# Two attention steps as one period with three row-tiled stretches, seven PSUM banks in one pool, early loads, and softmax sums inverted behind their own load

## The reference

```
xn = layernorm(x)                                  # over 256 features
q, k, v = split(xn @ w_qkv + b_qkv)                # 16 heads of width 16
scores  = q k^T / 4,  kept only where key >= query # a causal mask turned round
s = softmax(scores) v, heads joined, @ w_out + b_out
h = relu(s0 * [xn, -xn] @ W0) * 2                  # W0, W1, W2 hold +1 and -1
h = relu(s1 * h @ W1) * 2                          # 1024 wide
g = silu(s2 * h @ W2)                              # back to 256 wide
out = x + s * g
```

## Time and profile before

| | us |
|---|---|
| median of the 3 timed runs | 2762.31 |
| lowest, highest | 2743.96, 2768.26 |
| the profiled execution | 2761.34 |
| its span, first to last instruction | 2758.0 |

### The profile page before, as it was taken

How to read it: one execution, slowest core, us unless ns; L and a number is a source line. 1 busy time by engine, 2 the same in 40 slices (tenths; PEclk the granted TensorE clock), 3 DMA queues, 4 the chain that set the end, 5 groups by cost and what they waited for, 6 DMA issues and landing times.

```text
span 2758.0 us, 51670 instructions
## 1 busy us (share of the span) xinstructions
PE 2505.2 (91%) x17604; PEld 1506.8 (55%) x17604; DVE 1842.7 (67%) x4506; ACT 1538.7 (56%) x3123; POOL 931.2 (34%) x1095
## 2 busy tenths in 40 slices
PE   5984889999999899999899999999999999999985
PEld 4773555555555555555555555555555555555542
DVE  7762677777777666767667677777666776767630
ACT  3550355666666565656656565656565565656452
POOL 4002332333333424333433334342434333342532
PEclk8996899999999999999999999999999999999996
DMA  6982011111111202121211213021212112120321
GB/s 210 347 334 71 12 29 35 40 36 44 31 45 35 81 26 75 40 76 37 60 48 44 75 31 88 25 73 40 75 40 57 48 44 75 37 82 22 88 87 60
DMA packets 158109, 193.44 MB, mean 70 GB/s; under 512 B 65328, under 2 KB 102064, under 8 KB 157872
## 3 DMA queue, kind: packets, MB, share of 16 engines
q1 hardware_dynamic: 156912, 190.29, 22.6%
q10 hardware_dynamic: 960, 0.00, 0.0%
HBM read 112.60 MB, written 76.55 MB: 69 GB/s over the span
## 4 chain that ended last, share of the span: by engine, by line
PE 75%; ACT 4%; DMA 4%; SPq 3%; DVE 3%; issue 2%; POOL 1%; ACTq 0%; POOLq 0%
PE b_ps L977 19%; PE b_pv_ps L955 18%; PE b_ps L924 16%; PE b_ps L936 10%; PE b_ps L974 5%; PE b_ps L981 5%; DMA b_heads_T<-heads_T 3%; PE b_ps L999 3%; ACT b_probs L1015 2%; DVE b_part_max L1069 2%; SPq L757 1%; ACT b_u L1043 1%; SPq L724 1%; ACT b_sig L1035 1%; ACT b_z L1036 1%
## 5 line engine op out<-in xcount | busy, mean ns | idle before, releaser
L1015 ACT ACTIVATE b_probs<-b_ps 128x512 f32<-128x512 f32 (+3 forms) x2560 | 1224.8, 532 | 799.6 <-PE b_ps L924 799.1
L1069 DVE TENSOR_REDUCE b_part_max<-b_ps 128x1 f32<-128x512 f32 x1536 | 984.5, 682 | 347.7 <-PE b_ps L936 341.7
L1066 DVE CUSTOM_DVE_ANT_0 b_ps<-b_ps,k_mask 128x512 f32<-128x512 f32 (+3 forms) x1024 | 484.6, 515 | 328.7 <-PE b_ps L936 326.9
L924 PE MATMUL b_ps<-b_qst,k_kst 50*128 50x512 f32 (+3 forms) x2560 | 604.8, 467 | 62.4 <-ACT b_probs L1015 58.4
L955 PE MATMUL b_pv_ps<-b_probs,k_vst 128*32 128x512 f32 (+3 forms) x5120 | 616.1, 554 | 4.5 <-POOL b_probs L841 4.3
L924 PEld LDWEIGHTS b_ps<-b_qst,k_kst 50*128 50x128 f32 x2560 | 248.0, 186 | 630.2 <-ACT b_probs L1015 493.4
L936 PE MATMUL b_ps<-k_kst,b_qst 48*128 48x512 f32 (+3 forms) x2560 | 503.8, 385 | 82.6 <-DVE b_part_max L1069 61.1
L977 PE MATMUL b_ps<-b_u_hi,k_w 128*128 128x256 f32 x2048 | 541.1, 299 | 4.1 <-POOL b_u_lo L871 2.6
L977 PE MATMUL b_ps<-b_u_lo,k_w 128*128 128x256 f32 x2048 | 525.7, 292 | 0.0
L869 POOL CAST b_u_hi<-b_u 128x512 fp32r<-128x512 f32 x256 | 156.1, 610 | 828.3 <-ACT b_u L1043 827.9
L977 PEld LDWEIGHTS b_ps<-b_u_hi,k_w 128*128 128x128 f32 x2048 | 398.3, 195 | 64.8 <-issue 58.9
(11 more groups left out here) (87 smaller groups left out, 1908.6 us busy)
## 6 DMA issues: line engine op xcount, KB each, us to landing
qk_parts<-a_qk_parts SPq DMA_DIRECT2D x64, 512.0 KB, 3.1
b_qst<-qk_parts SPq DMA_DIRECT2D x384, 64.0 KB, 2.3
k_kst<-qk_parts SPq DMA_DIRECT2D x384, 64.0 KB, 2.2
a_xs<-L_attn_x SPq DMA_DIRECT2D x16, 512.0 KB, 5.8
xn_T<-a_xT SPq DMA_DIRECT2D x16, 512.0 KB, 6.1
v_plain<-a_v_out SPq DMA_DIRECT2D x16, 512.0 KB, 6.3
b_v_in<-v_plain SPq DMA_DIRECT2D x64, 128.0 KB, 2.6
b_xf<-xn_T SPq DMA_DIRECT2D x32, 256.0 KB, 3.4
```

What stands on the lines that cost most here:

```text
L924: pe.matmul(outs[half][:, 0:cols], keys, qst[rows, c, pair, 0:cols], start=True, stop=True).then_inc(s_ready, 1)
L1015: act.activation(probs[:, s % P_SLOTS, h, 0:cols], ps[:, banks[place, half][0], 0:cols], ACT.Exp, scale=HD ** -0.5).then_inc(exp_done, 1)
L1066: dve.tensor_tensor_reduce(src, src, mask[:, 0:CHUNK - k0 % CHUNK], 1.0, -3.0e38, ALU.add, ALU.max, dst).then_inc(ring_read, 1)
L1069: dve.tensor_reduce(dst, src, AX_X, ALU.max).then_inc(ring_read, 1)
```

## The change

**First stage.** The loop is written out. The sign matrices are converted by ACT, one per chunk from chunk 1 on, and by two DVE operations for W0; POOL clears `kst` at the very start, and the rest after the first `xT_low`. ACT copies the high parts before the v copies and the plain `xT` after them. Behind the q and k stores of chunk 13, SP loads the first xn piece and the k and q of group 0 for chunks 3 and 2 (24 DMAs) into buffers that both stages keep.

**Second stage.** Two steps (t even, t + 1) form a period. On PE it reads: S, M, S | F | M, S, M | PV of the odd step before | S, M | PV of the even step. F spans take some 19 matmuls at one place per period. All seven banks are one pool, in which F keeps its bank until its last span. The inversion waits for the sums alone and stands three steps behind the fetch (two for the last chunks), and P one step later than before. The last chunk's last group stays on chip: its sums are spread by a matmul, inverted and multiplied there, and projected by themselves.

```diff
@@ normalise_and_project, SP
+                if left == FIRST_LOADS:
+                    sp.wait_ge(xT_stored[0], 2 * DMA)
+                    sp.dma_start(kept.xf[:], scratch.xT[0, :, :, 0:PIECE]).then_inc(kept.x_loaded, DMA)
+                    for n in range(2):
+                        sp.wait_ge(qk_stored[n], 3 * QK_STORES * DMA)
+                    sp.wait_ge(blank, K_SLOTS)
+                    for c in LOADED_EARLY:
+                        load_parts(sp, scratch, 1, kept.kst[:, k_slot(c, 0)], K_PARTS, 0, c, kept.k_loaded[c])
+                        load_parts(sp, scratch, 0, kept.qst[:, c], Q_PARTS, 0, c, kept.q_loaded[c])
@@ POOL: conversions leave, clears move
-            for k in range(KF):
-                pool.tensor_scalar(kept.w1[:, k, :], k1s[:, k, :], 2.0, -1.0, ALU.mult, ALU.add).then_inc(w_ready, 1)
...
             for slot in range(K_SLOTS):
                 pool.memset(kept.kst[:, slot].bitcast(F32), 1.0).then_inc(blank, 1)
+            pool.wait_ge(xT_low, KH)
@@ ACT, end of a chunk
+                if left:
+                    copy_whole(i + 1, half + par, 1 - par)
+                if i > 0:
+                    convert(i - 1)
@@ order of the second stage
-PV_LAG, M_LEAD = 2, 21
+M_LEAD = 21
-S_POOL, D_POOL, F_POOL = (0, 1, 2), (3, 4, 5), (6,)
+BANKS = 7
+SCORE_PLACES = ((1.0, 1.2), (3.1, 5.0))
+MAX_PLACES = {4: (1.1, 3.0, 3.2, 5.1), 5: (1.1, 3.0, 3.2, 5.1, 5.2), 6: (0.9, 1.1, 3.0, 3.2, 5.1, 5.2)}
+VALUE_PLACES = (6.0, 4.0)
+NETWORK_PLACE = 2.0
...
-                out.append((t, 2.0 * pair, "S", n, s, pair))
+                out.append((period, SCORE_PLACES[t % 2][pair], "S", n, s, pair))
-                out.append((t + 1, 0.5, "mask", n, s))
-            out.append((t + PV_LAG, 3.0, "PV", n, s))
+                out.append((even(t), 0.5 if t % 2 else 2.5, "mask", n, s))
+            out.append((even(t), VALUE_PLACES[t % 2], "PV", n, s))
...
-    places = [(t, p) for t in range(-LEAD, 0) for p in (1.1, 3.05)]
-    places += [(t, 1.1) for t in range(GROUPS * STEPS - 12)]
+    places = [(t, p, 9) for t in range(-LEAD, 0, 2) for p in (2.0, 4.0, 6.0)]
+    left = total - sum(count for *_, count in places)
+    periods = range(0, GROUPS * STEPS - 12, 2)
+    places += [(t, NETWORK_PLACE, (n + 1) * left // len(periods) - n * left // len(periods))
+               for n, t in enumerate(periods)]
@@ combine
-COMBINE = (("fetch", 0), ("fetch_heads", 0), ("invert", 1), ("bias", 2), ("spread", 4), ("scale", 5),
-           ("project", 8))
+COMBINE = (("fetch", 0), ("fetch_heads", 0), ("bias", 2), ("invert", 3), ("spread", 5), ("scale", 6), ("project", 9))
...
-               (base + STEPS + PV_LAG + 1, NCHUNK - 4, COMBINE_LAST)]
+               (base + 35, NCHUNK - 4, COMBINE_LAST)]
...
+    out += [(base + 34, 3.9, "last_weights"), (base + STEPS + 2, 1.0, "last_sums")]
+    return out + [(base + STEPS + 2, 2.0 + half, "last_project", half) for half in range(2)]
@@ banks_of: one pool
-    free = {"exp": list(S_POOL), "ring": list(D_POOL), "f": list(F_POOL)}
+    free = list(range(BANKS))
...
+            if use not in out:
+                bank = free.pop(0)
+                counts[kind] += 1
+                out[use] = (bank, *last.get(bank, (None, 0)))
+                last[bank] = (kind, counts[kind])
+            if what != "F" or arg[8]:
+                free.append(out[use][0])
@@ DVE, invert
-                    dve.wait_ge(heads_fetched, (e + 1) * FETCHES * DMA)
-                    dve.reciprocal(sums[:], sums[:]).then_inc(inverted, 1)
+                    rows = slice(0, P if e < NCHUNK - 1 else LAST_HEADS * P // HEADS)
+                    dve.wait_ge(sums_fetched, (e + 1) * DMA)
+                    dve.reciprocal(sums[rows], sums[rows]).then_inc(inverted, 1)
@@ last group, DVE
+                elif what == "last_sums":
+                    src = ps[:, banks[place, 0][0]]
+                    for half in range(2):
+                        cols = slice(half * PIECE, (half + 1) * PIECE)
+                        dve.wait_ge(last_summed, 2)
+                        dve.reciprocal(heads_T[:, 0, cols], src[:, cols]).then_inc(last_inverted, 1)
+                        dve.wait_ge(last_inverted, half + 1)
+                        dve.tensor_tensor(sums_T[:, cols], sums_T[:, cols], heads_T[:, 0, cols], ALU.mult
+                                          ).then_inc(last_scaled, 1)
```

More of the change, by code:

```diff
@@ L89, in __init__, with load_parts @@
         self.vst = sb("vst", [P, CPB, TT, GH, VW])
+        self.qst = sb("qst", [P, CPB, PAIRS, CHUNK], F32R)
+        self.xf = sb("xf", [P, KH, PIECE])
+        self.q_loaded = [ctx.enter_context(nc.semaphore(f"k_q_loaded{c}")) for c in range(CPB)]
+        self.k_loaded = [ctx.enter_context(nc.semaphore(f"k_k_loaded{c}")) for c in range(CPB)]
+        self.x_loaded = ctx.enter_context(nc.semaphore("k_x_loaded"))
+def load_parts(sp, scratch, w, dst, parts, g, c, done):
+    b, gg = g // NG, g % NG
+    for r, part in enumerate(parts):
+        src = scratch.qk[w, b, c, gg * GW:(gg + 1) * GW, part]
+        src = src.rearrange("(p j d) n -> j d p n", j=HALVES, d=HD)
+        for j in range(HALVES):
+            row = j * HALF + r * HD
+            sp.dma_start(dst[row:row + HD].bitcast(F32), src[j]).then_inc(done, DMA)
 def normalise_and_project(nc, x, w_qkv, b_qkv, k0, k1, k2, s0, s1, s2, scratch, kept):
     LN_STEPS = 3
+    FIRST_LOADS = 2
     VU = TT // 2
@@ L160, in normalise_and_project, with over_chunks @@
         x_t = x.rearrange("b s h -> (b s) h")
-        def over_chunks(engine, chunk):
-            with engine.Fori(0, NCHUNK // 2 - 2) as pair:
-                for par in range(2):
-                    chunk(2 * pair + par, pair, par, 3)
-            for i in range(NCHUNK - 4, NCHUNK):
+        def over_chunks(chunk):
+            for i in range(NCHUNK):
                 chunk(i, i // 2, i % 2, NCHUNK - 1 - i)
@@ L486, in attention_events @@
     out = []
+    in_period = {}
+    for n in range(GROUPS):
+        for u in range(len(units)):
+            t = max_step(n * STEPS + u // PAIRS)
+            in_period.setdefault(t - t % 2, []).append((n, u))
+    place_of = {}
+    for t, those in in_period.items():
+        for place, (n, u) in zip(MAX_PLACES[max(4, len(those))], those):
+            place_of[n, u] = (t, place)
     for n in range(GROUPS):
@@ L510, in attention_events @@
             if n == 0 and what != "place_v":
+                if c in LOADED_EARLY and what != "load_v":
+                    continue
                 at = min(at, -LEAD - 1)
@@ L598, in banks_of @@
         kind, number = {"S": ("exp", HALVES), "M": ("ring", HALVES), "negmax": ("ring", 1), "fold_bias": ("ring", 1),
[L599 to L601 removed]
+                        "project": ("ring", 1), "last_sums": ("ring", 1), "last_project": ("ring", 1),
+                        "F": ("f", 1)}.get(what, (None, 0))
         for k in range(number):
[L603 to L607 removed]
+            use = ("F", arg[0]) if what == "F" else (at, k)
+            if use not in out:
[5 more added lines that the diff above has]
+                free.append(out[use][0])
     return out
@@ L715, in tokens @@
                 return a[i * CHUNK:(i + 1) * CHUNK, :].rearrange("(t p) h -> p t h", p=P)
-            def load_parts(w, dst, parts, g, c, done):
-                b, gg = g // NG, g % NG
-                for r, part in enumerate(parts):
-                    src = scratch.qk[w, b, c, gg * GW:(gg + 1) * GW, part]
-                    src = src.rearrange("(p j d) n -> j d p n", j=HALVES, d=HD)
-                    for j in range(HALVES):
-                        row = j * HALF + r * HD
-                        sp.dma_start(dst[row:row + HD].bitcast(F32), src[j]).then_inc(done, DMA)
             uses = 0
@@ L799, in _ @@
                     for h in range(PER):
-                        sp.dma_start(inv[h * HD:(h + 1) * HD], src[h].partition_broadcast(HD)).then_inc(inv_spread, DMA)
+                        n = KH if e < NCHUNK - 1 or PER + h < LAST_HEADS else 1
+                        sp.dma_start(inv[h * HD:(h + 1) * HD, 0:n], src[h, 0:n].partition_broadcast(HD)
+                                     ).then_inc(inv_spread, DMA)
+                elif what == "last_weights":
+                    sp.wait_ge(last_blank, 2)
+                    for h in range(GH):
+                        row = (LAST_HEADS + h) * HD
+                        sp.dma_start(wo_last[h * VW:h * VW + HD], w_out[row:row + HD, :]).then_inc(last_loaded, DMA)
+                elif what == "last_project":
+                    half, = arg
+                    rows = slice(half * FPU, (half + 1) * FPU)
+                    sp.wait_ge(y_ready, 2 * NCHUNK + half + 1)
+                    sp.dma_start(tokens(out_t, NCHUNK - CPB)[:, rows], xs[:, rows]).then_inc(y_stored, DMA)
                 elif what == "project":
```

255 lines of the change are left out of this document (157 added, 98 removed).

## The result

The changed kernel takes 2858.7 us (median of 4 runs, 2853.1 to 2862.9) against 2757.9 us for the kernel before (4 runs on the same chip): ratio 1.037, 95% interval 1.032 to 1.042. It is slower by 101 us where 205 less were forecast. The profiled execution took 2853.1 us.

A forecast was written before the change was run, and what follows sets the result against it. TensorE was taken as the bound, 76% of the span hanging on it. Terms -51, -62, -45, -11, -18 and -18 sum to -205 us, from 2761.3 to 2556 us; range 2490 to 2630.

The forecast's parts named there:

- part 6: Last group and tail: last chunk kept on chip saves DMA round trips; -18 us, between -35 and +5.
- Part 3: PSUM banks: one pool of seven removes half of about 85 us of PE waits for banks' readers; -45 us, 0 to -100.
- All fit, the last by 0.1: Walk through a full period: DVE frees every M pair's banks before PE needs them, the tightest by 0.1 us.
- DVE becomes the bound: Rival, chance 0.14: every S behind M waits for DVE, busy over 80%; Part 3 gives nothing, Part 1 half; 2626 us.
- Part 1: F stretches on PE: one per period instead of one per step, 268 fewer at 0.19 us each; -51 us.
- The 0.19: Cost in us that each F stretch on PE pays once, beyond 0.119 per matmul.
- Part 2: Inversion on DVE no longer waits for the heads, ending 12 stalls of PE and their slower clock; -62 us.
- Parts 4 to 6: First stage -11 us; start of the second stage -18 us; last group and tail -18 us.
- Part 4: First stage: second chunk starts earlier with POOL's conversions gone; -11 us, between -17 and 0.
- "slower" rival: Chance 0.04: with one pool, M pairs hold successors for DVE's full read; 3230 us, deciding from 0.34 us more per period.
- My test line: Middle of the run: periods near 6.8 us expected; the prediction is wrong if they stay at 7.1.

The follow-up runs named there:

- mask_early: Changed kernel with only the even steps' masks moved ahead of the network's splits and the combining's bias in GpSimd's order; 2663.1 us, ratio 0.963 to the kernel before.
- pv_later: Changed kernel with each PV, and the out and keep behind it, one period of two steps later; 2669.6 us, ratio 0.967 to the kernel before.
- f_merged: order_one_pool with the network's matmuls in one stretch of about 19 every second step instead of about 9 in each; 2730.8 us, ratio 0.990.
- half_max: mask_early with VectorE's reductions of M outside the diagonal blocks over 256 of their 512 columns; 2578.2 us, ratio 0.935.
- order_one_pool: Changed kernel without the two-step period: the hand-written order of before, with the one pool of seven banks; 2578.4 us, ratio 0.935.
- f_halves: order_one_pool with each step's network stretch of about 9 cut in two, the second between S and M of the second pair; 2788.2 us, ratio 1.012.
- old_order: Changed kernel with the hand-written order and the three bank pools of before; first stage, early loads, inversion and tail stay changed; 2653.9 us, ratio 0.962.
- before_invert: Kernel before with only the inversion changed: waits for its own load of the sums, three steps after the fetch; 2690.2 us, ratio 0.973.
- f_after_max: mask_early with each period's network stretch of 19 moved from ahead of the second M pair to behind it; 2809.9 us, ratio 1.020.
- three_pools: Changed kernel, keeping its two-step period, with the banks in three pools again (3, 3 and 1); 3716.0 us, ratio 1.346.

## Why the prediction was wrong

**The step that failed is one that isn't in it.** The prediction costed masks only at the end (part 6, "ahead of the last mask and the last PV"). In the period it followed PE, DVE and the banks, and never the path exp, mask, PV, though the change put PV into the same or the next period and set the even step's mask behind the splits of the network. A mask of 0.6 us waits there for pairs of splits of 1.9 each and for the combining's bias. mask_early prices this at 196 us, and pv_later, by the other end of the same path, at 189. Of the 185 us between the spans of the changed kernel and mask_early, 108 are idle time of PE and 77 are busy time; the matmuls are the same, and the clock is lower.

**Part 3, the pool (-45), by its walk-through.** The pool alone gives -85 in the old order and -75 in the changed kernel without the period: right in sign and too small. I took only half of the 85 us of waits as gained, and 85 and 75 are about all of them. In the period the walk-through, "All fit, the last by 0.1", failed. It took full widths and a DVE that starts each M at once. The trace has PV of 128 columns (0.43 instead of 1.0), M pairs bunched behind the stretch, masked reductions and reciprocals. S then waits 81 us in mask_early. The rival "DVE becomes the bound" named this wait, and with a chance of 0.14 I had it too low, as its own line for it ("the slack of 0.1") should have told. But its picture of VectorE was wrong: it has it busy for over 80%, and VectorE is busy for 62% of the span, in mask_early for 67%. What S waits for is single reads that come too late, not an engine without time. That its 2626 is near the 2663 of mask_early is in part chance.

**Part 1, fewer stretches (-51).** The size was about right: f_merged gives an estimated 60 us, and that half_max, whose stretches are merged, has 60 us less busy time on PE than order_one_pool (2388.7 and 2448.6) fits it. What part 1 lacked is the other side. A stretch is also the time in which exp and VectorE catch up, and without it in its old place PE waits: 152 us net lost in f_merged, and in half_max 63 us more idle time than in order_one_pool, which takes back the whole saving. The 0.19 holds for a stretch between M and S, where the kernel before has them. Between S and M it costs up to 0.40 (f_halves). The Trainium skill ("TensorEngine Tiling (Array Packing)", Key Properties) says that a change of tiling mode drains TensorE. For a stretch between S and M the traces agree, with 0.21 us lost beyond the 0.19, and there my reading that nothing more is to be had was wrong; for the stretches that this change took away it was nearly right.

**Part 2 (-62)** measured -70. **Parts 4 to 6 (-11, -18, -18)**: old_order is 104 us faster than before, less the 70 for the inversion that leaves 34 where 47 were forecast. In the changed kernel the start gained 15.6 and then 16.9 (27.2 after the stage's start, where it was 44.1), and the tail 16. The last group gives some back, as part 6 feared: from PV 600 to PV 640 old_order takes 174 us, the kernel before 160 and before_invert 153. Part 4 has the earlier trace rows agree that DVE is blocked for a whole instruction of POOL. That is less than they show: the 7.45 us go through some ten clears, of 0.9 and 0.5 us each. In the changed kernel four clears of 0.5 us run from 15.60 to 17.69 us beside the same operation of DVE on 4 columns, and it takes 0.35 us. That the second chunk comes earlier is measured; why DVE stood still for as long as 7.45 us stays open.

**The sum.** Parts 2 to 6 together were -154 and measured -182 (order_one_pool). The period was +280 instead of -51. Of these 196 are the masks. The 85 that are left are a net: waits for late reads of VectorE, which half_max prices at 85 with all that follows from them, and a last group that takes 19 us more, against the merge's saving and a start that is 9 us earlier. The merge's saving doesn't show beside the old order even in half_max, since other waits have taken its place; M, for one, waits 25 us for relu. The "slower" rival (0.04) named waits of S that hand on to ACT and PV and a limit of 0.34 us a period. Its mechanism was the smaller part (81 us of waits, 0.25 a period) and would not have turned the sign alone.

**My test line** was a poor one. I was wrong if the middle's period stayed at 7.1 us, and it did worse: from 600 to 2100 us PE has 9668 matmul records where it had 10403, and from PV 160 to PV 480 two steps take 8.1 us where they took 7.6, stalls included. But my own walk-through ends its full period at 7.07 (4.62 + 19 x 0.119 + 0.19), so the 6.8 that I gave as the forecast doesn't come out of it. By its median, order_one_pool with 7.08 would have failed the line too, and it is 182 us faster than the kernel before.

What stays open: half_max isn't below order_one_pool, though it gets through 11049 PE records from 600 to 2100 us and the other through 10951. The last 40 steps are where it loses: from PV 1 to PV 600 it takes 4 us less, from PV 600 to PV 640 17 more (184.4 and 167.0). This group has PV waits of 4.0 and 7.7 us for masks behind the combining, a wait of 8.0 us for relu, and 3 to 7 us of P for the heads that GpSimd scales; no kernel moved those alone. Nor was the pool's 85 us divided among the waits that it removes, and no kernel has the early masks and the later PV together.

## What to carry to other kernels

When an order is rewritten by hand, walk each consumer's whole path, through the engine that is idle most of the time as well: what counts is what stands ahead in its queue when the short operation becomes due. Merging work of one kind to save switches also removes the pauses in which the other engines catch up; count how many units the ring of buffers reaches back (here three pairs) and ask, at each place, whether the reader of that unit has been served, at the narrow widths as at the full ones. And look at the clock beside idle time of TensorE, because its price differs: 108 us of idle time in the changed kernel came with 77 us of slower matmuls, and the idle time of f_merged and f_after_max came with almost none (below).

## What the runs showed of the hardware that I had not expected

- The same idle time can cost clock or not. From 600 to 2100 us PE of the changed kernel waits 143 us, of which 89 are in 43 waits of 1.0 to 4.7 us, and the granted clock is 0.92 to 0.95. Without the late masks (mask_early: 78 us, 8 waits over 1.0) it is 0.98 to 1.00. f_after_max waits 136 us and f_merged 121, all in waits under 1.0 us, and their clock is 0.99 or 1.00. A stretch of f_merged, in which PE is busy for the same 275.4 us as in the changed kernel, whose clock there is 0.93:
```profile
900.00:1200.00 300.00, 275.39 (x2066) 163.04 (x2066) 206.68 (x512) 177.62 (x367) 108.59 (x128) 1.00 0.19 54
```
  That short waits are always free isn't shown either: in three_pools 433 waits, 30 of them over 1.0 us, add up to 289 us, and the clock is 0.79 to 0.90. Behind one wait of 2.20 us a stretch of 19 matmuls took 4.09 us instead of 2.43.
- M to S can take less than the single case in the rows of before suggests. In f_after_max it is 0.23 or 0.24 us in 68 of 70 full-width cases of the middle (708.10 to 708.34), where the earlier trace rows have 0.32; in mask_early it is 0.34 more often than 0.24. S of 128 columns holds PE 0.16 us in order_one_pool and often only 0.06 to 0.13 in mask_early. A stretch between S and M makes both of them hold PE longer, 0.40 in place of 0.19 in all.
